# Scan loop of a 12-sublayer decoder: B rows read from SBUF instead of spread into PSUM, and a second pair of decay banks

## The reference

```python
def _mamba(x, in_proj_w, conv_w, conv_b, x_proj_w, dt_proj_w, dt_proj_b, A_log, D, out_proj_w):
    x_in, z = jnp.split(jnp.einsum('bld,ed->ble', x, in_proj_w), 2, axis=-1)
    x_in = _silu(causal_depthwise_conv(x_in, conv_w) + conv_b)
    dbc = jnp.einsum('bld,ed->ble', x_in, x_proj_w)
    delta_in = dbc[..., :D_INNER]
    Bp = dbc[..., D_INNER:D_INNER + D_STATE]
    Cp = dbc[..., D_INNER + D_STATE:]
    delta = jax.nn.softplus(jnp.einsum('bld,ed->ble', delta_in, dt_proj_w) + dt_proj_b)
    A = -jnp.exp(A_log)
    def step(h, inp):
        dt, bt, ct, xt = inp
        dA = jnp.exp(dt[:, :, None] * A[None])
        h = dA * h + dt[:, :, None] * bt[:, None, :] * xt[:, :, None]
        y = jnp.einsum('bds,bs->bd', h, ct) + D * xt
        return (h, y)
    _, y = jax.lax.scan(step, h0, (delta, Bp, Cp, x_in))   # over the tokens
    return jnp.einsum('ble,de->bld', y * _silu(z), out_proj_w)
```

## Time and profile before

| | |
|---|---|
| median of 3 runs | 2431.88 us (2419.36 to 2435.54) |
| the profiled execution | 2436.99 us, of which the profile's span is 2435.2 us |
| TensorE busy in the span | 2029.0 us (83%) |
| VectorE busy | 1439.2 us (59%) |
| ScalarE busy | 939.1 us (39%) |
| GpSimd busy | 789.1 us (32%) |
| scan loop | from about 1730 us to about 2221 us of the span |
| mean granted clock of TensorE | 0.93 of full speed |

### The profile page before, as it was taken

The page is one execution under the profiler, slowest core; times in us unless marked ns, Lnnn a source line. Parts: engine busy times, 40 slices in busy tenths (PEclk is TensorE's granted clock), DMA queues, the critical chain, the costliest instruction groups (busy, mean ns, idle before and its releaser), DMA issues. The chain is left out here.

```text
span 2435.2 us, 37168 instructions
## 1 busy us (share of the span) xinstructions
PE 2029.0 (83%) x14090; PEld 1450.0 (60%) x14107; DVE 1439.2 (59%) x2859; ACT 939.1 (39%) x1548; POOL 789.1 (32%) x559
## 2 busy tenths in 40 slices
PE   7998766873995896499677878998998989788998
PEld 5775544662985785499444664685343434355887
DVE  3886884576323566211473555235799899999333
ACT  3433423431111343133333431113776666655443
POOL 1221231234002100100323013204588798978200
PEclk8999988996998786799888999999999999999999
DMA  5217001002995110699200002394211110300000
GB/s 166 79 41 260 24 32 39 2 19 87 349 380 199 37 33 9 258 349 354 90 1 27 2 2 110 96 271 117 83 36 35 31 40 2 116 9 1 9 9 18
DMA packets 104577, 232.65 MB, mean 96 GB/s; under 512 B 10000, under 2 KB 77456, under 8 KB 95568
## 3 DMA queue, kind: packets, MB, share of 16 engines
q1 hardware_dynamic: 95664, 208.24, 24.6%
q0 software_dynamic: 7680, 20.98, 2.7%
q10 hardware_dynamic: 1056, 1.05, 0.1%
HBM read 174.27 MB, written 55.97 MB: 95 GB/s over the span
## 5 line engine op out<-in xcount | busy, mean ns | idle before, releaser
L4095 POOL TENSOR_TENSOR l_attn_ring<-l_attn_ring,l_attn_c_rows 128x1024 f32<-128x1024 f32 x128 | 301.4, 2355 | 78.9 <-DVE l_attn_ring L3907 78.9
L3907 DVE TENSOR_TENSOR_SCAN l_attn_ring<-bank,l_attn_ring 128x512 f32<-128x512 f32 x256 | 299.1, 1210 | 21.2 <-ACT bank L3711 16.7
L3467 PE MATMUL bank<-l_attn_ring,identity 128*128 128x512 f32 x512 | 244.3, 599 | 17.7 <-POOL l_attn_ring L4095 14.3
L3711 ACT ACTIVATE bank<-l_attn_step,l_attn_minus_exp_a_log 128x508 f32<-128x508 f32 x256 | 173.7, 685 | 153.2 <-DVE l_attn_ring L3907 152.7
L170 PE MATMUL bank<-x_features,weights 128*128 128x512 f32 x416 | 200.7, 622 | 15.4 <-ACT l_attn_silu_z L3625 4.9
L3467 PEld LDWEIGHTS bank<-l_attn_ring,identity 128*128 128x128 f32 x512 | 95.6, 192 | 125.1 <-issue 98.5
L3901 DVE TENSOR_TENSOR l_attn_ring<-l_attn_step_times_input,bank 128x1024 f32<-128x1024 f32 x128 | 153.4, 1198 | 3.4 <-PE bank L3453 1.6
L487 DVE TENSOR_REDUCE negmax_slots<-bank 128x16 f32<-128x2048 f32 x48 | 109.8, 2287 | 74.3 <-PE bank L374 73.8
L170 PEld LDWEIGHTS bank<-x_features,weights 128*128 128x128 f32 x416 | 79.3, 197 | 107.3 <-issue 88.2
L179 PE MATMUL bank<-weights,x_features 128*128 128x256 f32 (+1 forms) x336 | 99.5, 452 | 7.8 <-ACT weights L3741 3.3
L468 ACT ACTIVATE l_xattn_probs<-bank 128x2048 f32<-128x2048 f32 x32 | 60.1, 1877 | 99.0 <-PE bank L374 99.0
(11 more groups left out here) (729 smaller groups left out, 4444.2 us busy)
## 6 DMA issues: line engine op xcount, KB each, us to landing
l_attn_tile_weights<-l_ffn_experts SPq DMA_DIRECT2D x22, 2180.0 KB, 9.7
ffn_experts_tile_weights<-l_ffn_experts_experts SPq DMA_DIRECT2D x37, 1024.0 KB, 8.6
expert_slots<-zeros SPq DMA_DIRECT2D x8, 2048.0 KB, 11.6
l_attn_c_rows<-state_outputs SPq DMA_DIRECT2D x64, 256.0 KB, 3.3
l_ffn_tile_weights<-l_ffn_experts SPq DMA_DIRECT2D x23, 512.0 KB, 4.5
expert_slots<-residual_sum SPq DMA_DIRECT2D x62, 128.0 KB, 8.8
expert_slots<-zeros SPq DMA_DIRECT2D x1, 5888.0 KB, 27.7
l_ffn_tile_x<-expert_slots SPq DMA_DIRECT2D x23, 256.0 KB, 4.1
```

Of the source, the lines that this page charges most:

```text
L3467: mm = pe.matmul(net.banks[SUMS[j]][:], net.ident[:], ring[n % 4][:, j, :], start=s == 0, stop=s == STATES - 1)
L3711: nc.scalar.activation(by_seq(net.banks[DECAY[j]][:])[:, :, 1:], by_seq(dt[:, m, :])[:, :, 1:], ACT.Exp, scale=a[:, m * STATES + s:m * STA ...
L3907: nc.vector.tensor_tensor_scan(ring[n % 4][:, j, :], net.banks[DECAY[j]][:], ring[n % 4][:, j, :], 0.0, ALU.mult, ALU.add).then_inc(state_ ...
L4095: tt(ring[n % 4][:], ring[n % 4][:], c_row[:, n % STATES, :].unsqueeze(1).broadcast_to([P, 2, T]), ALU.mult).then_inc(out_ready, 1)
```

## The change

- The B and C rows of a group are copied out of PSUM once (`take_bc`, now one copy on ScalarE), stored to DRAM side by side for each state (`store_rows`, two DMAs a group) and loaded together, 4 KB repeated on 128 partitions, 512 KB in SBUF, once for each of the 128 units, into a ring of eight slots (`b_and_c`, `rows_loaded`). A slot is loaded again when GpSimd's multiply of eight units before is done.
- VectorE's drive waits for the slot (`wait_rows`) and reads the B row from it in SBUF. GpSimd's multiply reads the C row from the same slot.
- TensorE's `spread_b`, the bfloat16 parts, ScalarE's `middle_part` and `low_part` and GpSimd's `rest` are gone.
- Banks 6 and 7 become a second pair for the decays, so that the exponentials of unit n wait for the scans of unit n-2.
- SyncE's queue is written as one loop over the 128 units, with the stores of the next group at at = 26 and the loads of the last layer's weights and of the context at fixed places between. The banks of the feed-forward part and of the last output are renamed to fit.

The diff, cut to its core:

```diff
-        c_row = sb("c_rows", [P, STATES, T])
+        b_and_c = sb("b_and_c_rows", [P, ROW_SLOTS, 2, T])
...
-        SUMS, DECAY, SIDE, B_ROW = (0, 1), (2, 3), (4, 5), (6, 7)
+        SUMS, DECAY, SIDE = (0, 1), ((2, 3), (6, 7)), (4, 5)
...
+        def row(n, k):
+
+            return b_and_c[:, n % ROW_SLOTS, k, :].unsqueeze(1).broadcast_to([P, 2, T])
+
+        def wait_rows(engine, n):
+
+            engine.wait_ge(rows_loaded[n % ROW_SLOTS], 16 * (n // ROW_SLOTS + 1))
...
                 def begin_last_y():
 
-                    pe.wait_ge(drive_ready, total)
+                    pe.wait_ge(state_ready, 2 * (total - 1))
...
-                def spread_b(n):
-                    if n >= 2:
-                        pe.wait_ge(drive_ready, n - 1)
-                    spread_out(net.banks[B_ROW[n % 2]], n // UNITS, n % STATES).then_inc(b_in_psum, 1)
...
                     if g:
-                        act.wait_ge(bc_ready, g)
-                    if g >= 2:
-                        act.wait_ge(b_in_psum, UNITS * (g - 1))
-                    nc.scalar.copy(bc[g % 2][0:rows_, :], src).then_inc(part_ready, 1)
-                    nc.scalar.copy(bc_rest[0], src).then_inc(taken, 1)
+                        act.wait_ge(rows_stored, 32 * g)
+                    nc.scalar.copy(bc, src).then_inc(taken, 1)
...
-                        if n:
-                            act.wait_ge(state_ready, 2 * n + j - 1)
-                        nc.scalar.activation(by_seq(net.banks[DECAY[j]][:])[:, :, 1:],
+                        if n >= 2:
+                            act.wait_ge(state_ready, 2 * (n - 2) + j + 1)
+                        nc.scalar.activation(by_seq(net.banks[DECAY[n % 2][j]][:])[:, :, 1:],
                                              by_seq(dt[:, m, :])[:, :, 1:], ACT.Exp,
                                              scale=a[:, m * STATES + s:m * STATES + s + 1]).then_inc(decay_ready, 1)
...
                 def unit(n):
                     g, half_ = n // UNITS, n % UNITS // STATES
-                    dve.wait_ge(b_in_psum, n + 1)
+                    wait_rows(dve, n)
                     dve.wait_ge(dtu_ready, DT_ * g + 2 * half_ + 2)
                     if n >= 4:
                         dve.wait_ge(summed, n - 3)
-                    tt(ring[n % 4][:], dtu[:, 2 * half_:2 * half_ + 2, :],
-                       net.banks[B_ROW[n % 2]][:].unsqueeze(1).broadcast_to([P, 2, T]),
-                       ALU.mult).then_inc(drive_ready, 1)
+                    tt(ring[n % 4][:], dtu[:, 2 * half_:2 * half_ + 2, :], row(n, 0), ALU.mult).then_inc(drive_ready, 1)
...
-                    if n % UNITS < STATES:
-                        wait_c(pool, g * STATES + n % STATES)
-                    tt(ring[n % 4][:], ring[n % 4][:],
-                       c_row[:, n % STATES, :].unsqueeze(1).broadcast_to([P, 2, T]), ALU.mult).then_inc(out_ready, 1)
+                    wait_rows(pool, n)
+                    tt(ring[n % 4][:], ring[n % 4][:], row(n, 1), ALU.mult).then_inc(out_ready, 1)
...
-                        if at in (17, 20):
-                            rest(g + 1, (at - 17) // 3)
...
+                def store_rows(g):
                     sp.wait_ge(taken, number["bc", g, 0] + 1)
+                    for k in range(2):
+                        sp.dma_start(net.state_rows[g, :, k, :], bc[STATES * k:STATES * (k + 1), :]).then_inc(
+                            rows_stored, 16)
+                    sp.wait_ge(rows_stored, 32 * (g + 1))
+
+                store_rows(0)
+                for n in range(total):
+                    g, at = divmod(n, UNITS)
+                    if at == 26 and g + 1 < GROUPS:
+                        store_rows(g + 1)
...
+                    if n >= ROW_SLOTS:
+                        sp.wait_ge(out_ready, n - ROW_SLOTS + 1)
+                        wait_rows(sp, n - ROW_SLOTS)
+                    rows = net.state_rows[g, n % STATES].rearrange("k t -> (k t)").unsqueeze(0)
+                    sp.dma_start(b_and_c[:, n % ROW_SLOTS, :, :].rearrange("p k t -> p (k t)"),
+                                 rows.broadcast_to([P, 2 * T])).then_inc(rows_loaded[n % ROW_SLOTS], 16)
```

More of the change, by code:

```diff
@@ L3232, in l3_decoder @@
         ex, positive = sb("exp_minus_abs", [P, DT_, T]), sb("positive_part", [P, DT_, T])
-        c_row = sb("c_rows", [P, STATES, T])
+        b_and_c = sb("b_and_c_rows", [P, ROW_SLOTS, 2, T])
         ring = [sb(f"ring{i}", [P, 2, T]) for i in range(4)]
-        PARTS = 6 * STATES
-        rest_room = net.ctx_room[1][:].rearrange("p b d -> p (b d)")
-        bc_rest = [rest_room[0:2 * STATES, i * T:(i + 1) * T] for i in range(2)]
-        part = sb("b_and_c_part", [2 * STATES, T], BF16)
-        bc = [sb(f"b_and_c_parts{i}", [PARTS, T], BF16) for i in range(2)]
-        pick = sb("pick_row", [PARTS, 2 * STATES], BF16)
+        bc = net.ctx_room[1][:].rearrange("p b d -> p (b d)")[0:2 * STATES, 0:T]
         a = sb("minus_exp_a_log", [P, DT_ * STATES])
@@ L3296, in l3_decoder @@
         xs = Parts(*(rounded["conv_silu"][2][:, i, :, :] for i in range(2)))
-        h0 = Parts(*([rounded["c_rows"][:, 8 * i + m, :] for m in range(8)] for i in range(2)))
+        h0 = Parts(*([rounded["b_and_c_rows"][:, 8 * i + m, :] for m in range(8)] for i in range(2)))
         h1 = Parts([room[:, m, :] for room in (rounded["silu_z"], rounded["conv_silu"][0]) for m in range(4)],
@@ L3578, in _ @@
                     step_project(0, m)
-                pe.wait_ge(tables_ready, 1)
-                for n in range(2):
-                    spread_b(n)
                 net.keep_running(pe, net.banks[SUMS[0]], 15)
                 for n in range(total):
-                    if n + 2 < total:
-                        spread_b(n + 2)
                     ends = n % STATES == 0
@@ L3911, in _ @@
                 dve.wait_ge(net.ready["l3_attn"], 16)
-                for k in range(3):
-                    chain.step(nc.vector.tensor_copy(pick[rows_ * k:rows_ * (k + 1), :], net.ident[0:rows_, 0:rows_]))
                 def arrive(g):
@@ L3952, in _ @@
                         weights_of_step.wait_taken(dve)
-                        for j in range(2):
-                            chain(nc.vector.memset(by_seq(net.banks[DECAY[j]][:])[:, :, 0], 0.0))
+                        for j in range(4):
+                            chain(nc.vector.memset(by_seq(net.banks[DECAY[j // 2][j % 2]][:])[:, :, 0], 0.0))
                         nc.vector.engine_nop().then_inc(tables_ready, 1)
@@ L4086, in _ @@
                 for m in range(2):
-                    rest(0, m)
                     lost_part(0, m)
@@ L4165, in _ @@
-                for g in range(2, GROUPS):
-                    sp.wait_ge(filled, number["kv", g - 2, NB - 1] + 1)
-                    net.load_ctx(sp, g, net.ctx_room[g % 2], ctx_in[g - 1])
+                    if g == GROUPS - 1 and at in (12, 18):
+                        of = 2 + (at - 12) // 6
+                        sp.wait_ge(filled, number["kv", of - 2, NB - 1] + 1)
+                        net.load_ctx(sp, of, net.ctx_room[of % 2], ctx_in[of - 1])
+                    if n >= ROW_SLOTS:
+                        sp.wait_ge(out_ready, n - ROW_SLOTS + 1)
+                        wait_rows(sp, n - ROW_SLOTS)
```

68 lines of the change are left out of this document (15 added, 53 removed).

## The result

The changed kernel takes 2501.86 us (median of 6 runs, 2496.79 to 2514.12) against 2433.71 us for the kernel before (6 runs). The ratio is 1.0305, with a 95% interval from 1.028 to 1.0331: slower by 3%. The profiled execution after has a span of 2512.3 us, 77.1 more than before.

What follows compares the result with a forecast made beforehand. Three nearly full engines bound the loop, with VectorE gapless at 3.48 us a unit in steady state. Span 2435.2 + 73.7 (loop) - 2.8 (start) = 2506.1 us; the median, 3.3 lower, gives 2503 us, range 2475 to 2560 (80%).

Steps and rivals of the forecast that it cites:

- What excludes what (part 3): In the loop, VectorE's drive (turn 1.10 us) and GpSimd's multiply (2.32) can't overlap; side instructions block 1.22, tensor_scalar 0.41.
- The rival without blocking (2403): Drives in the loop run beside GpSimd as before; loop 465.2 us, total 2403 us; chance 5%.
- The rival in which side instructions block 0.41 us each (2439): In the loop only GpSimd's multiply excludes the drive; side instructions block 0.41 us each; total 2439 us; chance 5%.
- The order (part 4): In the loop the next unit's drive precedes GpSimd's multiply by 0.16 us; units without side work stay at 3.48 us.
- Side units of tensor_tensor, 4.64 us: 78 loop units with a GpSimd tensor_tensor side instruction: 1.10 + 2.32 + 1.22 = 4.64 us each, 361.9 us.
- the lower bound (0.13 us a unit): In the loop, part of a waiting multiply's work may be hidden: 0.13 us a unit, 128 x 0.13 = 17 us less.
- Side units of tensor_scalar, 3.83 us: 16 loop units with a GpSimd tensor_scalar: 1.10 + 2.32 + 0.41 = 3.83 us each, 61.3 us.
- Other work of VectorE (part 5): Where VectorE has gates or statistics between scans and drive, GpSimd's multiply mostly goes first; together 23.4 us added.
- part 7: Before the loop, two stores and a load bring the first drive at about 1727.3: -2.8 us, bounds -5 and +3.
- The rows (part 6): 128 row loads of 512 KB, about 1.6 us of the DMA engines each, eight slots of lead: priced at nothing.
- the 0.70 at which it would have decided: TensorE's granted clock bounds the loop only below a mean of 0.70; at 0.6 2636 us; chance 3%.
- it was cover, as priced: TensorE's 128 dropped spreading matmuls in the loop, 49.0 us of busy time, hidden under VectorE's 3.48 us: priced at nothing.

Runs made afterwards that it cites:

- The late drive: The changed kernel with two 128x1 VectorE instructions added ahead of each drive, which start 0.36 us before it: 2690.04 us against 2425.84, ratio 1.108.
- the kernel with ScalarE's copies between the decays: Changed kernel's loads, one pair of decay banks, ScalarE copying each B row to PSUM for the drive between a unit's two decays: 2422.47 us against 2430.79, ratio 0.9962.
- the kernel with the cut side work: The changed kernel with most GpSimd side instructions from the second group on cut to 16 columns: 2435.69 us against 2425.84, ratio 1.0041.

## Why the prediction was right

The forecast was 2503 us, the measurement is 2501.86. By steps:

- *What excludes what (part 3).* Right, and shown by experiment from both sides: one operand in SBUF makes the loss in the kernel before, one operand in PSUM takes it out of the kernel after. The rival without blocking (2403) fell with the first; with the drive in PSUM its time nearly came true, 2411.5. The rival in which side instructions block 0.41 us each (2439) fell with the units of 4.52 us.
- *The order (part 4).* Right: the drive goes first by 0.16 us, units without side work stay at 3.49. The late drive shows that this was a close thing, worth 188 us.
- *Side units of tensor_tensor, 4.64 us.* Measured 4.52. The drive's turn is 4.52 - 2.32 - 1.22 = 0.98 us rather than 1.10: the start of the instruction that waits is already done when its turn comes. The prediction had this as the lower bound (0.13 us a unit) and did not take it. Over some 70 units, 8 us too many.
- *Side units of tensor_scalar, 3.83 us.* This term was mis-sized. The four tensor_scalar of group 2 make units 10 to 14 take 3.51, 4.35, 4.49, 4.49 and 4.49 us, together 21.3, where 4 x 3.83 + 3.48 = 18.8 had been priced: 0.6 us too few for each. 14 of the 16 delay a unit of the loop (the last two come behind the last drive), so some 8 us were missing. I had let the next drive begin while the tensor_scalar was finishing. The first of a row does let the drive through, and more than I had priced (GpSimd's timeline, then VectorE's):

```profile
2051.21 2.26 POOL L3344 TENSOR_SCALAR x_tokens<-residual_sum,ln_mean_var,ln_rstd 128x256 f32<-128x256 f32 x1
```

```profile
2051.31 1.23 DVE L3868 TENSOR_TENSOR l_attn_ring<-l_attn_step_times_input,l_attn_b_and_c_rows 128x1024 f32<-128x1024 f32 x1
```

  The tensor_scalar starts 0.10 us ahead of the drive. The drive takes 1.23 us all the same, and it is the tensor_scalar that waits, 2.26 us instead of 1.23. This happens at all three rows of tensor_scalar in the loop, here and in the six other runs with a drive from SBUF, side work of full width and no added delay: 21 cases, leads of 0.08 to 0.10 us, drives of 1.23 to 1.25. A tensor_tensor over 128x512 with such a lead holds the drive for its whole length, as at 1742.11 above. But GpSimd's queue is then late, and from the second unit on the drive meets the multiply instead. VectorE's and GpSimd's timelines:

```profile
2269.91 2.20 DVE L3868 TENSOR_TENSOR l_attn_ring<-l_attn_step_times_input,l_attn_b_and_c_rows 128x1024 f32<-128x1024 f32 x1
2272.15 2.34 DVE L3872 TENSOR_TENSOR_SCAN l_attn_ring<-bank,l_attn_ring 128x512 f32<-128x512 f32 x2
2274.40 2.20 DVE L3868 TENSOR_TENSOR l_attn_ring<-l_attn_step_times_input,l_attn_b_and_c_rows 128x1024 f32<-128x1024 f32 x1
```

```profile
2268.69 2.34 POOL L4046 TENSOR_TENSOR l_attn_ring<-l_attn_ring,l_attn_b_and_c_rows 128x1024 f32<-128x1024 f32 x1
2271.02 2.19 POOL L3344 TENSOR_SCALAR x_tokens<-residual_sum,ln_mean_var,ln_rstd 128x256 f32<-128x256 f32 x1
2273.18 2.34 POOL L4046 TENSOR_TENSOR l_attn_ring<-l_attn_ring,l_attn_b_and_c_rows 128x1024 f32<-128x1024 f32 x1
```

  The drive (2269.91) waits for a multiply that ends at 2271.03. The tensor_scalar then waits for the drive, and the multiply behind it on GpSimd follows at once, before the next drive is there (2274.40). However long the tensor_scalar would block, GpSimd's own queue runs it and the multiply one after the other, so the 0.41 us doesn't enter in these units. The rule of whole blocking on the page "SBUF — State Buffer" of the Trainium skill, section "Who interferes with whom", gave 2516 with the same sum. The later units lie near it (4.49 against 4.64 us), but that is no test of it, since the queue alone explains them. The first unit of each row goes against it: the instruction that was issued first did not block. Here the measurement decides, and the rule holds in this case for tensor_tensor but not for this tensor_scalar.
- *Other work of VectorE (part 5).* Behind the unit at at = 17 the multiply does go ahead of the drive, as predicted, but I had booked the wait one unit early. In groups 1 to 3 the unit at at = 17 takes 5.81 us (predicted 5.90), which is 3.49, 1.30 for the gates and 1.03 for a side instruction; the agreement is luck. The wait is in the record of the next drive, so the unit at at = 18 takes 8.23, 8.20 and 10.49, against 7.12, 7.12 and 8.35, and the two units behind it come out short (4.43 and 3.49 in group 1, against 4.64 each). Over these four units of group 1 it is 21.96 us against 22.30. In group 0, without a side instruction before them, the units at 17 and 18 take 4.78 and 4.59. Not foreseen were the group's ends. There the order turns over too:

```profile
1858.62 2.34 DVE L3872 TENSOR_TENSOR_SCAN l_attn_ring<-bank,l_attn_ring 128x512 f32<-128x512 f32 x2
...
1860.75 1.26 POOL L4016 TENSOR_TENSOR l_attn_step_times_input<-l_attn_step,l_attn_conv_silu 128x512 f32<-128x512 f32 x1
...
1861.98 2.34 POOL L4046 TENSOR_TENSOR l_attn_ring<-l_attn_ring,l_attn_b_and_c_rows 128x1024 f32<-128x1024 f32 x1
1862.10 3.30 DVE L3868 TENSOR_TENSOR l_attn_ring<-l_attn_step_times_input,l_attn_b_and_c_rows 128x1024 f32<-128x1024 f32 x1 [1.15 <-issue]
```

  (The timeline of all engines.) VectorE stands idle for 1.15 us. The profile names no releaser, but the code does: the first drive of a group waits for `dtu_ready`, that is for GpSimd's `step_times_input` (L4016), which ends at 1860.75 + 1.26 = 1862.01. In the kernel before this wait is 0.44 us. GpSimd goes straight on to its multiply, 0.12 us ahead of the drive. The units at at = 31, 0 and 2 then take 5.74, 5.59 and 5.5 instead of 4.64, those at 1 and 3 come out shorter than priced (4.79, 3.49): together 25.1 us against 24.5.
- *The sum.* 564.9 us predicted for the loop, 570.1 measured; the first drive predicted at 1727.3, measured at 1726.86. The two terms of side units, 8 too high and 8 too low, nearly cancel; the rest is the group's ends and the first units. So the hit within 2 us is better than its parts, and two more steps were luck. The span came out at 2512.3, 6.2 above the 2506.1 predicted, and the median lies 10.4 us under it, where 3.3 had been taken: the profiled run is the slowest of the six. And the first drive moves from profile to profile: in the ten that begin as the changed kernel does it lies between 1712.87 and 1728.85, so the gain of 3 us at the start (part 7) is neither shown nor refuted.
- *The rows (part 6).* Right: 128 loads landed in 3.6 us at the median, 9.2 at most, and VectorE is shown to have waited for none of them. The stores took 3.1 us at the median, where one store had taken 3.6 before. The 1.6 us of the DMA engines for a load is borne out too: their mean busy share in the loop is 0.35, and 0.35 x 570 / 128 = 1.56 us.
- *TensorE.* I had expected 49 us less of busy time. The windows over the whole loop, of the kernel before (the columns are those of the earlier trace rows):

```profile
1730.00:2221.00 491.00, 449.89 (x1191) 209.84 (x1192) 461.57 (x436) 314.10 (x456) 415.47 (x226) 0.98 0.12 38
```

  and after:

```profile
1727.00:2297.00 570.00, 455.31 (x1070) 201.26 (x1068) 560.27 (x437) 307.10 (x445) 518.44 (x219) 0.93 0.35 122
```

  It is busy for 455 us with 121 matmuls fewer, 54 us more than I had expected. While it waited for GpSimd's multiplies (97.0 us) the granted clock of the loop fell from 0.98 to 0.93, and the mean matmul of `add_up` went from 599 to 658 ns, 512 x 0.059 = 30 us; the rest of the 54 was not taken apart. This was off the path (in the loop VectorE waited 4.5 us for sums before the change and not at all after), and far from the 0.70 at which it would have decided. In the kernel with ScalarE's copies between the decays the spreading is gone too, and it gains 0.4% in all: it was cover, as priced.

## What to carry to other kernels

Before an operand of VectorE is moved from PSUM to SBUF, look in the trace for what GpSimd does at that moment, and for any place where VectorE already has two SBUF inputs beside it: here two instructions after the loop told the outcome of 128 in it. The price is not the operand's but the order's: as long as the two turns fit under one period and the shorter instruction comes first, exclusion is free; each further GpSimd instruction is added nearly in full, and a start later by a few tenths of a microsecond can cost 2.4 us in every unit. A copy on an engine with room that brings the row to PSUM can be cheaper than reading it where it lies.

## What the runs showed of the hardware

- A GpSimd tensor_scalar over 128x256 that starts 0.08 to 0.10 us ahead of a drive doesn't hold it (drive 1.23 to 1.25 us, tensor_scalar 2.26 instead of 1.23), while a tensor_tensor over 128x512 with about the same lead does (drive 2.2).
- A drive of VectorE that starts 0.03 us behind GpSimd's multiply waits for all of it (3.39 us instead of 1.20), in the kernel with the cut side work.
- An instruction that waits for its turn has its start behind it: the sum of the three turns in a unit is 4.52 us, where the instructions alone, from start to start, take 1.23 (1752.20 to 1753.43), 2.32 and 1.22, 4.77 in all.
- A waiting drive is not always next. Behind a GpSimd subtract over 32 partitions with one bfloat16 input it was passed over until GpSimd had nothing left, 6.87 us instead of 2.2, in three groups of each of two kernels.
- Between drive and multiply the order is settled anew in each unit, by who starts first after the scans: in the kernel with the late drive, where that is GpSimd each time, nearly all units take 5.88 us. In the changed kernel the order came back wherever VectorE reached its drive straight from the scans.
